# A two-layer transformer on one core: where the mixer's raw weights and the KAN coefficients are loaded

## The reference, cut to what matters

```
mod = silu(L1_c) @ L1_wmod          # sa, ca, ga, sb, cb, gb for each sequence
h = layernorm(x) * (1 + ca) + sa    # the modulating stage
out = layernorm(h) * ln1_g + ln1_b
out_f = mamba(out, in_proj, conv_w_f, x_proj_f, dt_w_f, A_log_f, D_f, out_proj)
out_b = mamba(out reversed, ... the _b weights ...), reversed back
out = layernorm(out_f + out_b) * ln_g + ln_b
y[n,j] = sum_ik cos(k*out[n,i])*coef[0,j,i,k] + sin(k*out[n,i])*coef[1,j,i,k]   # k = 1..8, the KAN
x = x + ga * (y + h)
x = x + gb * experts(layernorm(x) * (1 + cb) + sb)
```

## Time and profile before

| | |
|---|---|
| median of 3 runs | 3874.04 us (3861.91 to 3876.59) |
| the profiled execution | 3872.47 us |
| its span, first to last instruction | 3870.0 us |
| mean granted TensorE clock | 0.824 of full speed |
| busy: PE / DVE / ACT / POOL | 2824.0 / 2925.6 / 1969.2 / 2072.3 us |
| DMA | 286.02 MB, mean 74 GB/s |

### The profile page before, as it was taken

The page is one execution under the profiler, slowest core; times in us unless marked ns, Lnnn a source line. Parts: engine busy times, 40 slices in busy tenths (PEclk is TensorE's granted clock), DMA queues, the critical chain, the costliest instruction groups (busy, mean ns, idle before and its releaser), DMA issues. The chain is left out here.

```text
span 3870.0 us, 54204 instructions
## 1 busy us (share of the span) xinstructions
PE 2824.0 (73%) x16586; PEld 1927.1 (50%) x16587; DVE 2925.6 (76%) x4205; ACT 1969.2 (51%) x3140; POOL 2072.3 (54%) x1348
## 2 busy tenths in 40 slices
PE   3999999632999950578787777777777777649944
PEld 2455555331666630255555454555555544549944
DVE  3788887470444456299999999999999999947744
ACT  1566666430333310477766666777666666312232
POOL 1011111175222212498888888988888899502225
PEclk6899999555999975778888888898888888669965
DMA  3444444321111143132333333333333333121050
GB/s 95 85 89 87 87 87 87 99 78 46 39 39 39 38 123 92 39 85 74 80 85 80 81 80 81 77 77 81 83 80 80 80 82 80 47 78 26 22 147 20
DMA packets 224516, 286.02 MB, mean 74 GB/s; under 512 B 33356, under 2 KB 135782, under 8 KB 219418
## 3 DMA queue, kind: packets, MB, share of 16 engines
q1 hardware_dynamic: 212034, 264.40, 29.3%
q0 software_dynamic: 12256, 18.82, 1.4%
HBM read 236.57 MB, written 54.22 MB: 75 GB/s over the span
## 5 line engine op out<-in xcount | busy, mean ns | idle before, releaser
L1691 POOL TENSOR_TENSOR resid_x<-s_ux,s_B_rows 128x1024 f32<-128x1024 f32 x512 | 1204.7, 2358 | 216.7 <-PE s_y L1938 215.5
L1884 DVE TENSOR_TENSOR_SCAN resid_x<-s_dA,resid_x 128x1024 f32<-128x1024 f32 x512 | 1170.9, 2287 | 80.9 <-ACT s_dA L1752 77.7
L1752 ACT ACTIVATE s_dA<-s_dt,s_A 128x510 f32<-128x510 f32 x1024 | 662.0, 678 | 424.4 <-DVE resid_x L1884 421.8
L1938 PE MATMUL s_y<-identity,resid_x 128*128 128x128 f32 x4096 | 652.5, 312 | 0.0
L1938 PEld LDWEIGHTS s_y<-identity,resid_x 128*128 128x128 f32 x4096 | 587.0, 164 | 99.2 <-issue 69.1
L1892 DVE TENSOR_TENSOR resid_x<-resid_x,s_C 128x1024 f32<-128x1024 f32 x512 | 615.0, 1201 | 7.6 <-PE s_C L1928 7.6
L1928 PE MATMUL s_C<-s_bc_parts,s_w_sel 96*128 96x512 bf16 x512 | 230.0, 449 | 403.2 <-DVE resid_x L1892 400.7
L467 DVE TENSOR_REDUCE a_row_max<-a_maxscores 128x2 f32<-128x512 f32 x512 | 336.2, 683 | 83.7 <-PE a_maxscores L545 83.4
L1928 PEld LDWEIGHTS s_C<-s_bc_parts,s_w_sel 96*128 96x128 bf16 x512 | 51.2, 100 | 602.3 <-DVE resid_x L1892 572.3
L391 ACT ACTIVATE a_probs<-a_scores 128x1024 f32<-128x1024 f32 x256 | 262.7, 1026 | 146.4 <-PE a_scores L558 142.1
L1223 POOL DMA_INDIRECT choice_outputs<-e_y,e_idx x135 | 131.0, 970 | 340.2 <-DVE e_y L1208 339.9
(11 more groups left out here) (318 smaller groups left out, 4975.8 us busy)
## 6 DMA issues: line engine op xcount, KB each, us to landing
s_B_rows<-b_rows SPq DMA_DIRECT2D x256, 512.0 KB, 4.9
a_Q<-split_qk SPq DMA_DIRECT2D x96, 192.0 KB
split_qk<-a_parts SPq DMA_DIRECT2D x32, 384.0 KB, 2.8
e_x<-slot_inputs SPq DMA_DIRECT2D x135, 65.0 KB, 1.8
a_K<-split_qk SPq DMA_DIRECT2D x64, 128.0 KB
f_mod_rows<-mod_rows SPq DMA_DIRECT2D x16, 512.0 KB, 7.2
c_y<-choice_outputs SPq DMA_DIRECT2D x16, 512.0 KB, 6.5
a_K<-split_qk SPq DMA_DIRECT2D x32, 192.0 KB
```

Source lines behind the costliest of these rows:

```text
L1691: tt(R[:, s % 4, d], ux[par][:, d], bsb[s % BRING][:, d].unsqueeze(1).broadcast_to([P, C2, W]), ALU.mult).then_inc(S["in_ready"], 1)
L1752: last = func(dA[:, d, c2, :, lo:lo + T - 1], dt[par][:, d, c2, :].rearrange("p (g t) -> p g t", t=T)[:, :, lo:lo + T - 1], ACT.Exp, scale ...
L1884: nc.vector.tensor_tensor_scan(r, a, r, 0.0, ALU.mult, ALU.add).then_inc(S["scanned"], 1)
L1938: last = mm(YP[:, t, c2 * P:(c2 + 1) * P], R[:, s % 4, d, c2, t * P:(t + 1) * P], core.ident[:], is_transpose=True, start=(c == 0 and t % ...
```

## The change

The 23 loads of raw weights are now issued by ACT, inside the block of the modulating stage, through a new argument of `modulated`. The issue order and the shapes stay as they were. `mixer_weights` only waits for them. The buffers for the raw weights and the tables are therefore allocated ahead of the modulating stage. The load of the KAN coefficients is now issued by SP in the read-back's block, ahead of the read-back of x, into a buffer that stays until the end of `kan`. All semaphores and waits on the data are kept.

```
-def modulated(core, layer, Hr, L, row):
+def modulated(core, layer, Hr, L, row, load_beside=None):
...
+            if load_beside is not None:
+                @block.scalar
+                def _(act):
+                    load_beside(act)
...
+def load_mixer_raw(core, eng, raw, Wt, loaded):
+    aps = core.aps
+    def load(dst, src, **how):
+        eng.dma_start(dst, src, **how).then_inc(loaded, 16)
+    load(raw["win"][:], aps["L1_attn_in_proj_w"].rearrange("(c p) e -> p c e", p=P))
+    load(raw["wout"][:], aps["L1_attn_out_proj_w"])
+    load(raw["sel"][:], aps["selector"])
+    for d, f in enumerate("fb"):
+        ... (the nine loads of a direction, as before)
+    load(Wt["ln1"][:, 0:1], ...)
+    load(Wt["ln1"][:, 1:2], ...)
...
-def mixer_weights(core, Wt, on):
+def mixer_weights(core, Wt, raw, loaded):
...
-            @block.sync
-            def _(sp):
-                ... (the 23 loads)
             @block.scalar
             def _(act):
-                act.wait_ge(S["loaded"], loads)
+                act.wait_ge(loaded, 16 * RAW_LOADS)
...
             @block.vector
             def _(dve):
-                dve.wait_ge(S["loaded"], loads)
+                dve.wait_ge(loaded, 16 * RAW_LOADS)
...
-def kan_weights(core, WT, const):
+def kan_weights(core, WT, const, coef, s_in):
...
-            @block.sync
-            def _(sp):
-                sp.dma_start(coef[:], aps["L1_attn_kan_coef"].rearrange("p j i k -> j p (i k)")).then_inc(s_in, 16)
...
-        modulated(core, 1, Hr, None, 8)
+                modulated(core, 1, Hr, None, 8, lambda act: load_mixer_raw(core, act, raw, Wt, raw_loaded))
                 norm_stats(core, "lnC1", 1e-12)
+                mixer_weights(core, Wt, raw, raw_loaded)
+            mixer(core, Hr, OD, x_saved, Wt)
+        coef, coef_loaded = core.sbuf("kw_coef", [P, 2, D * GRID], on=on), core.sem("kw_loaded")
         with core.nc.Block() as block:
             @block.sync
             def _(sp):
+                sp.dma_start(coef[:], core.aps["L1_attn_kan_coef"].rearrange("p j i k -> j p (i k)")).then_inc(coef_loaded, 16)
                 sp.dma_start(core.X[:, 0:core.NT * D], xsave).then_inc(x_back, 16)
```

More of the change, by code:

```diff
@@ L1489, with mixer_tables @@
            22: [("step_size", 1, 0)], 23: [("times_x", 1, 0), ("less_exp", 1, 1)], 24: [("less_off", 1, 1)], 25: [("step_size", 1, 1)], 26: [("times_x", 1, 1)]}
-def mixer_weights(core, Wt, on):
+def mixer_tables(core, on):
+    sb = lambda name, shape, dt=F32: core.sbuf("s_" + name, shape, dt, on=on)
+    return {"taps": sb("w_taps", [P, DIRS, C2, DC, P]), "z": sb("w_z", [P, C2, P]), "out": sb("w_out", [P, C2, P]),
+            "bc": sb("w_bc", [P, DIRS, C2, 2 * BC]), "dt": sb("w_dt", [P, DIRS, C2, C2, P]), "sel": sb("w_sel", [PARTS * BC, BC, P], BF16),
+            "skip": sb("w_skip", [P, DIRS, C2, P]),
+            "A": sb("A", [P, DIRS, C2, DS]), "conv_b": sb("conv_b", [P, DIRS, C2, 1]), "dt_b": sb("dt_b", [P, DIRS, C2, 1]),
+            "D": sb("D", [P, DIRS, C2, 1]), "ln1": sb("ln1", [P, 2]), "one": sb("one", [P, 1]), "minus_one": sb("minus_one", [P, 1])}
@@ new lines, in mixer_raw @@
+def mixer_raw(core, on):
+    sb = lambda name, shape, dt=F32: core.sbuf("w_" + name, shape, dt, on=on)
+    return {"win": sb("in_proj", [P, 4, D]), "wout": sb("out_proj", [P, DI]), "sel": sb("selector", [PARTS * BC, BC]),
+            "taps": sb("conv_w", [P, DIRS, C2, DC]), "xp": sb("x_proj", [BC + DTR, DIRS, DI]), "xdt": sb("x_proj_dt", [DTR, DIRS, DI]),
+            "dtT": sb("dt_w_T", [DTR, DIRS, DI]), "alog": sb("A_log", [P, DIRS, C2, DS])}
+RAW_LOADS = 3 + DIRS * 9 + 2
+def load_mixer_raw(core, eng, raw, Wt, loaded):
[6 more added lines that the diff above has]
+    for d, f in enumerate("fb"):
+        load(raw["taps"][:, d], aps[f"L1_attn_conv_w_{f}"].rearrange("(c p) k -> p c k", p=P))
+        x = aps[f"L1_attn_x_proj_w_{f}"]
+        load(raw["xp"][0:DS, d], x[DTR + DS:DTR + BC])
+        load(raw["xp"][DS:BC, d], x[DTR:DTR + DS])
+        load(raw["xdt"][:, d], x[0:DTR])
+        load(raw["dtT"][:, d], aps[f"L1_attn_dt_w_{f}"].rearrange("d r -> r d"), allow_slow_non_contiguous=True)
+        load(raw["alog"][:, d], aps[f"L1_attn_A_log_{f}"].rearrange("(c p) s -> p c s", p=P))
+        for name in ("conv_b", "dt_b", "D"):
+            load(Wt[name][:, d], aps[f"L1_attn_{name}_{f}"].rearrange("(c p n) -> p c n", p=P, n=1), allow_slow_non_contiguous=True)
+    load(Wt["ln1"][:, 0:1], aps["L1_attn_ln1_g"].rearrange("(p n) -> p n", n=1))
+    load(Wt["ln1"][:, 1:2], aps["L1_attn_ln1_b"].rearrange("(p n) -> p n", n=1))
@@ L1496, in mixer_weights @@
     with tmp:
[L1497 to L1506, removed]
+        win, wout, sel, taps, xp, xdt, dtT, alog = (raw[n] for n in ("win", "wout", "sel", "taps", "xp", "xdt", "dtT", "alog"))
+        scaled = core.sbuf("w_in_taps", [P, DIRS, C2, DC, D], on=tmp)
         ps = core.psum("w_ps", [P, 4, 512], on=tmp)
-        S = {n: core.sem("w_" + n) for n in ("loaded", "scaled", "ps", "kept", "exp_done", "bc_zeroed")}
-        names = "fb"
+        S = {n: core.sem("w_" + n) for n in ("scaled", "ps", "kept", "exp_done", "bc_zeroed")}
         jobs = []
@@ L1591, in _, with mixer @@
                         nc.tensor.matmul(ps[:, n % 4, 0:P], src, rhs, start=True, stop=True).then_inc(S["ps"], 1)
-def mixer(core, Hr, OD, x_saved):
+def mixer(core, Hr, OD, x_saved, Wt):
     nc, B, aps = core.nc, core.B, core.aps
@@ L1602, in mixer @@
         sb = lambda name, shape, dt=F32: core.sbuf("s_" + name, shape, dt, on=on)
[L1603 to L1608, removed]
         PADW = T + 2 * (DC - 1)
@@ L2072, in kan_weights @@
     with tmp:
-        coef = core.sbuf("kw_coef", [P, 2, D * GRID], on=tmp)
         comb = core.sbuf("kw_combined", [P, NBASIS, D], on=tmp)
@@ L2076, in kan_weights @@
         ps = core.psum("kw_ps", [P, NBASIS // 4 + 1, 512], on=tmp)
-        s_in, s_comb, s_ps, s_wt, s_const = (core.sem(f"kw_{n}") for n in ("loaded", "combined", "ps", "kept", "const"))
+        s_comb, s_ps, s_wt, s_const = (core.sem(f"kw_{n}") for n in ("combined", "ps", "kept", "const"))
         with nc.Block() as block:
-            @block.sync
-            def _(sp):
-                sp.dma_start(coef[:], aps["L1_attn_kan_coef"].rearrange("p j i k -> j p (i k)")).then_inc(s_in, 16)
             @block.vector
@@ L2112, in _, with kan @@
                 nc.tensor.matmul(ps[:, NBASIS // 4, 0:D], minus2[:], WT[:, B_EE, :], start=True, stop=True).then_inc(s_const, 1)
-def kan(core, Hr, OD, x_back):
+def kan(core, Hr, OD, x_back, coef, coef_loaded):
     nc, NT, X, aps = core.nc, core.NT, core.X, core.aps
@@ L2123, in kan @@
         WT, const = sb("coef_T", [P, NBASIS, D]), sb("constant", [P, D])
-        kan_weights(core, WT, const)
+        kan_weights(core, WT, const, coef, coef_loaded)
         ln = sb("ln_cols", [P, 2])
@@ L2298, in _ @@
                 sp.dma_start(xsave, core.X[:, 0:core.NT * D]).then_inc(x_saved, 16)
-        norm_stats(core, "lnC")
-        modulated(core, 1, Hr, None, 8)
-        norm_stats(core, "lnC1", 1e-12)
-        mixer(core, Hr, OD, x_saved)
+        tables = ExitStack()
+        with tables:
+            Wt = mixer_tables(core, tables)
+            read = ExitStack()
+            with read:
+                raw, raw_loaded = mixer_raw(core, read), core.sem("w_loaded")
+                norm_stats(core, "lnC")
+                modulated(core, 1, Hr, None, 8, lambda act: load_mixer_raw(core, act, raw, Wt, raw_loaded))
+                norm_stats(core, "lnC1", 1e-12)
+                mixer_weights(core, Wt, raw, raw_loaded)
+            mixer(core, Hr, OD, x_saved, Wt)
+        coef, coef_loaded = core.sbuf("kw_coef", [P, 2, D * GRID], on=on), core.sem("kw_loaded")
         with core.nc.Block() as block:
@@ L2305, in _ @@
             def _(sp):
+                sp.dma_start(coef[:], core.aps["L1_attn_kan_coef"].rearrange("p j i k -> j p (i k)")).then_inc(coef_loaded, 16)
                 sp.dma_start(core.X[:, 0:core.NT * D], xsave).then_inc(x_back, 16)
         norm_stats(core, "lnC2", 1e-12)
-        kan(core, Hr, OD, x_back)
+        kan(core, Hr, OD, x_back, coef, coef_loaded)
 def adaln_two_layers(nc, aps, B):
```

## The result

Timed in 7 runs each, the changed kernel took 3843.54 us (3833.64 to 3847.99) and the kernel before 3868.07 us (3861.91 to 3876.59): a ratio of 0.9935, 95% interval 0.9922 to 0.9948, 24.5 us faster. Six later timings of it, against ten of the kernel before, gave 0.9936 (0.9916 to 0.9956). The forecast of 3849 us lies 5.5 us above the median and the range held it.

The account below looks back on a forecast made before the run. DVE bounds the mixer and PE the KAN, both untouched; the change targets transfer waits that move the end one for one. 3872.47 - 15.7 + 2.7 - 10.8 = 3848.7, given as 3849 us, range 3838 to 3861.

Parts of the forecast that it names:

- Part 1: Mixer's start: weight loads leave SP's block, so DVE starts when SP used to issue, 15.7 us gained.
- the bound that was named: Mixer's start: DVE's first operation 0.59 us after the one ahead, at 1536.39, making the gain 0.1 us less.
- Part 2: Modulating stage: ACT's loads delay the modulation rows, costing 2.7 us, between 0 and 8.
- the first rows: Modulating stage's start: DVE's 10.2 us wait grows by 1.7 us, as ACT's loads share the DMA engines.
- the refills: Modulating stage's steady part: about five refills land later beside ACT's remaining loads, costing 1.0 us.
- the bound of 8: Modulating stage: upper end of the loads' cost, 8 us, against a lower end of 0.
- signs of being wrong: Rows' wait growing over 5 us, more than the first few refills stalling DVE, or coefficients' wait above 3 us.
- Part 3: Read-back's block: coefficients issued earlier and ahead of x, so DVE uses them sooner, 10.8 us gained.
- A: Modulating stage: first rows wait for all DMA time and refills stall, costing 8 us; 3854 us; chance 0.20.
- B: Read-back: coefficients land with x despite the order on SP, gaining nothing there; 3859.5 us; chance 0.08.
- C: Modulating stage: bound by its loads throughout, every refill landing in 10.8 us, costing 38 us; 3884 us; chance 0.04.

Follow-up runs that it names:

- the whole: The changed kernel with both halves, weight loads on ACT and coefficients ahead of x, against the kernel before: 3843.54 us, ratio 0.9935.
- the weights alone: The kernel before with only the 23 weight loads issued by ACT in the modulating stage, coefficients loaded as before: ratio 0.9979.
- x first: The changed kernel with x's read-back issued ahead of the coefficients in the same block: 13.89 us from the third norm's first operation to their first use.
- the repeat: The changed kernel, unaltered, run once more against the kernel before: ratio 0.9936.
- the coefficients alone: The kernel before with only the coefficients loaded ahead of x in the read-back's block, the 23 loads staying on SP: ratio 0.9986.
- one load a step: The changed kernel with ACT issuing one load after each modulating step, first to 23rd: 72.77 us from the save's issue to the second norm.

## Why the prediction was right

**Part 1** gave 15.64 us against 15.7. DVE started 0.1 us later than SP had issued before, the bound that was named.

**Part 2** was forecast at 2.7 us, as 1.7 for the first rows and 1.0 for the refills, and came out at 4.55; 3.4 to 4.6 in the four traces with the loads at this place. The direction and the bound of 8 held. The waits grew by 5.01 us, of which 4.55 show in the length of the stage: 3.05 in the first three waits, for the first four loads of rows, and 1.96 in those for refills. Both terms came out at nearly twice their size. Two of the prediction's own signs of being wrong were reached: the wait grew by 5.01 us, where the limit was 5, and five refills stalled DVE, up to step 9, which is more than the first few.

The step that failed is the pricing by engine time and bytes. The loads were counted as 5.8 us of work of which the rows pay a share. What they paid for was the number of elements of two 8 KB loads; with the same bytes in long runs 0.5 us of waits are left behind the first. The prediction also counted only the wait for the first rows, though the other three of the first four loads stood beside ACT's loads too.

By the rule of the Trainium skill, "DMA: Bandwidth & Descriptors", section "Queues, rings and completion order", that an engine alternates between the queues that have work, the first rows would have paid 0.6 us, an estimate. The first wait alone, from the first normalization to the first rows' use, grew by 1.2 us in the whole, 1.0 in the weights alone, 0.2 with x first and -0.2 in the repeat, where the coefficients alone, with nothing added there, gave -0.4; that fits 0.6. The other two waits of the first loads, 1.15 to 1.84 us in these four traces, have no place in that estimate. Alternation packet by packet doesn't show in what the profile records. From 1469 to 1473 us SP's queue (q1) and ACT's (q10) moved nearly the same number of packets, but from 1475 to 1480 us, behind the first dt_w load, ACT's moved more than three times as many:

```profile
q1 hardware_dynamic: 470, 0.22, 19.7%
q10 hardware_dynamic: 475, 0.21, 18.5%
```

```profile
q10 hardware_dynamic: 1523, 0.06, 70.6%
q1 hardware_dynamic: 437, 0.21, 46.8%
```

No run here tells what one record of a packet stands for. How single elements hold up the rows is therefore not shown; shown is that the stalls go when the elements are joined. The Trainium skill's sentence that a second issuer saves only the usually small issue time ("DMA: Bandwidth & Descriptors", "Issuing engines are not separate DMA queues") did not hold in size: 15.6 us saved, 4.6 paid.

**Part 3** gave 10.33 us against 10.8. From issue to use it took 4.9 us, where 4.4 were worked out (3402.7 to 3407.1); of these 0.15 are a slip, since 3403.2 + 2.75 is 3405.95 and not 3406.1. By the 6.15 us for 1 MB of the Trainium skill ("DMA: Bandwidth & Descriptors", "Bandwidth") it would have been 1.7 us later than forecast; it was about 0.5. SP's second issue in that block, priced at nothing, goes with a third norm 0.56 us later; with the read-back a block later the norm came earlier again and the coefficients were used no sooner, so the delay is hidden behind their landing. The read-back cost nothing, as forecast: POOL started with its block.

**Not in the sum** was the tables' block, 1.96 us longer. Windows of this block before and after (PE and PEld busy first, the granted clock third from the end):

```profile
1559.00:1561.00 2.00, 2.00 (x11) 1.69 (x10) 2.00 (x11) 0.00 (x0) 0.00 (x0) 0.50 0.03 8
1561.00:1565.00 4.00, 3.90 (x27) 3.33 (x26) 3.89 (x21) 0.00 (x0) 0.00 (x0) 0.92 0.00 0
```

```profile
1543.00:1547.00 4.00, 3.91 (x18) 3.21 (x19) 4.00 (x20) 0.00 (x0) 0.00 (x0) 0.50 0.01 4
1547.00:1551.00 4.00, 4.00 (x20) 3.94 (x19) 2.45 (x12) 0.00 (x0) 0.00 (x0) 0.50 0.00 0
```

Before, PE's clock rose to 2.4 GHz inside the block; after, it stayed at 1.2 GHz. The 16 small dt matmuls took 299 ns each before and 451 after, and DVE, which had copied their results without a wait before, waits for them after:

```profile
1562.87 0.52 DVE L1579 COPY s_w_dt<-w_ps 128x128 f32<-128x128 f32 x2
```

```profile
1548.71 0.72 DVE L1595 COPY s_w_dt<-w_ps 128x128 f32<-128x128 f32 x2 [0.25 <-PE w_ps L1607]
```

Up to the last copy of the taps' products the block took 9.9 us in both. The longer block doesn't always come with the loads on ACT: with one load a step it took 13.9 us again.

**The rivals.** A (8 us in part 2) and B (coefficients with x) did not come: 4.55 us, and a wait of 0.2. C needed landing times of 9.1 us in all refills; the median was 4.7 in the changed kernel.

**Luck.** The mechanism held in parts 1 and 3, and in part 2 by direction. The closeness of the number is luck. The four touched stretches make 19.5 us where the prediction's sum has 23.8, so it gave 4.3 too many: 2.0 for the tables, 1.9 for part 2, 0.5 for part 3. With the measured stretches it would have said 3853.0. Against that, its start, the profiled execution's 3872.47 us, lies 4.4 above the median of the seven timings, and the timed gain exceeds the stage sum by 5.1 us for which no cause is shown. The three errors together leave the 5.2 us between 3848.7 and 3843.5.

## What to carry to other kernels

When 23 small loads are waited for at the head of a block, look at who issues them: the issue took 14 us, and an idle engine can do it in the block ahead. Count the elements of what you move there, not the bytes: two loads of 8 KB that transpose element by element held up the loads beside them, and reading them in rows gave back 3 to 4 us of a cost of 3.4 to 4.6. And put what is needed first ahead of the large transfer in the same queue: the order alone brought 10.3 us, the earlier issue nothing.

## What the hardware showed that was not expected

- The DMA share was 0.83 at 72 GB/s with ACT's loads beside the refills and 0.36 at 71 GB/s without them. The recorded time of the packets grew by about 9 us, more than the 5.8 us of all the loads alone, and the share went over 1 (1.17 from 1475 to 1480 us), so it is no measure of work where two queues meet.
- ACT's issue of the load behind a 2048-element load took 8.03, 5.49, 6.04 and 4.02 us in different company, 2.11 once ACT had waited for the save, 2.02 alone, and 0.40 when the elements were contiguous. The price of those elements shows as the issue time of the load behind.
- The granted clock of the same 40 PE instructions in the tables' block went to 1.00 in the last 3 us in some traces and stayed at 0.50 in others, so that the block took 13.9 us in three traces (before, coefficients alone, one load a step) and 15.9 us in eight (the whole, its repeat, weights alone and others). PE had been idle for 150 us ahead of it before, 137 with one load a step and 139 in the whole. In the three traces with dt_w by rows, which have four more PE instructions there, the clock rose in two (after 133 and 135 us of idle time; 14.7 and 15.2 us) and stayed in one (after 132 us; 16.7 us). Nothing tried here tells what decides it.
